# GpSimd's row sends moved between its variance sums and its root guess, in the first graph stage of a four-layer kernel

## Chip, cores and metric

One core of one Trainium2 chip runs the whole program in one launch. The metric is device time in microseconds of one execution, smaller is better.

## The reference, cut to what matters

Four layers follow each other on x of shape (32, 256, 128): a graph layer with 4 heads, a routed feed-forward layer (top 2 of 8 experts per token), a second graph layer, and a second routed layer. Each adds its output to x. The change is in the first graph layer and in the hand-over of its result to the routed layer.

```python
x = x + _L0_gnn_ref(_layernorm(x, axis=-1), adj, ...)
x = x + _L0_ffn_ref(_layernorm(x, axis=-1), L0_ffn_Wg, ...)
...
# _L0_gnn_ref
X = _heads(lrelu(node_feats @ W_lin + b_lin), B, N)
q = _heads(lrelu(node_feats @ W_q), B, N)
k = _heads(lrelu(node_feats @ W_k), B, N)
att = sigmoid(einsum('bhxd,bhyd->bhxy', q, k) * scale)
adj_h = adj_matrix[:, None] * att
deg = sum(adj_h, axis=-1)
dis = where(deg > 0, deg ** (-0.5), 0.0)
Y = einsum('bhxy,bhyd->bhxd', dis[..., :, None] * adj_h * dis[..., None, :], X)
return layernorm(Y) * ln_g + ln_b
# _L0_ffn_ref
gate_scores = x @ Wg + bg
_, idx = jax.lax.top_k(gate_scores, 2)
```

## The kernel before, in words

All engines' programs are written out by hand; semaphores alone order them. The first graph stage is a software pipeline over the 32 batches of 256 nodes (two tiles of 128 rows, TB = 2). It runs slots s = -5 to 31. In slot s, batch s gets its scores and its weighted adjacency matrix, while other batches stand at other steps: batch s-2 its output, s-4 its attention term added to x, s-6 its normalised rows, s-7 its gates.

Names that the prediction uses, by engine.

- VectorE (DVE), `gnn0_vector`. Its order in a slot is the body of the loop over s: `xd` (L937) and `xs` (L944) weigh the values; `veps` (L956) takes the degrees; `adj_h` (L908, twice) weighs the adjacency matrix; `y_sb` (L951) weighs the output; `kqT` (L919) finishes keys and queries. Between them the generator `solve_steps` is advanced by `next(steps)`. It turns variances and degrees of the slot before into reciprocal roots for all three layer norms and the degrees at once, on tiny tiles of 16 columns: `newt` (L865, L868), `near` and `far` (L871, L872, L875), `rstd` (L884), `dis` (L887), `shift` (L891). A second generator, `picks`, is advanced beside it: the choice of two experts per token and the row numbers of a group (`gmax`, `place`, `chosen`, `pair`, `emask`, `row_of`). The `bn_stats` (L897) measure mean and variance of two tiles each: of the input batch s+5, of `y_sb` of batch s-2, and of the rows of batch s-4 after the attention term was added (`AT_R`, written to `stats` from `xres`).
- GpSimd (POOL), `gnn0_gpsimd`. In each slot: `sums_of_stats` (seven ops of 8 or 16 columns: `mdiff`, `sqsum`, `mdiff`, `sqsum`, `veps`, `guess`, `msum`, L1242 to L1255) once the slot before has all its statistics; then `send` of one tile; then `add_attention` (three ops of 256 columns on `y_n` and `xres`, L1226, L1229, L1232); then `send` of another tile. DVE's `newt` L865 waits for `guess`; its `bn_stats` of the rows of batch s-4 wait for `add_attention`.
- A send (L1262) is an indirect DMA: 128 normalised rows from `rows` go to the places `row_of` in the DRAM tensor `pair_rows`. A group is four batches, so eight tiles in four parts of two. The groups 0 to 3 are sent one part per slot: tile 0 of the part behind the attention term of one slot, tile 1 ahead of the attention term of the next. Group 4 (IN_DRAIN - 1) is sent four tiles at a time at the end of slots 30 and 31. Groups 5 and up follow after the loop.
- ScalarE (ACT), `gnn0_scalar`, takes the sigmoid of the scores in two halves (`psum`, L687), normalises, and copies results out of PSUM (`yT` L693, `deg` L727 and others). TensorE (PE) does scores (L431), output (L493, L519), degrees (L542, L579) and values (L506).

The order around the change, as written:

```python
for s in range(FIRST, NB):
    if s > 0:
        sums_of_stats(s)
    for g, part in second_tiles(s):
        send(g, part, [1])
    if batch(s - 4):
        add_attention(s - 4)
    for g, part in sends(s):
        send(g, part, [0] if g < IN_DRAIN - 1 else range(TB))
```

## Time and profile before

| | us |
|---|---|
| median of 3 runs | 714.55 (712.74 to 719.56) |
| the profiled execution's own time | 719.42 |
| its span | 717.6 |
| PE busy in the span | 633.6 (88%) |
| DVE busy | 531.4 (74%) |
| ACT busy | 471.8 (66%) |
| POOL busy | 363.3 (51%) |

The busy times are of the whole span; the first graph stage takes about its first 265 us, and the shares there differ. A row of the timeline gives the start in us from the span's start, the duration in us, the engine, the line, the operation, output and inputs with their shapes, and in brackets the idle time before it with what ended it. Where several instructions of a line follow each other, one row holds them all (x2). Starts of consecutive DVE rows lie a little closer than the durations, since the end of one overlaps the start of the next.

### The profile page before, as it was taken

To read this page: it belongs to the slowest core of one execution; us is meant where nothing else is said; L and a number is where in the kernel's file an instruction comes from. 1 tells how busy PE (TensorE), PEld (TensorE's weight loads), DVE (VectorE), ACT (ScalarE), POOL (GpSimd) and SP (SyncE) were. 2 spreads that over 40 slices of the span, in tenths; PEclk is the share of its full clock that TensorE was granted. 3 is DMA by queue.
4 is the path that set the end of the run, shared out by engine and by line. 5 is a ranking of instruction groups with operands and counts; after the bars stand their busy time and mean duration, and the time that the engine had idled before them with its cause. 6 is when DMAs were issued, how large, how long until landed. Compare 5 with 4: busy or idle time off the path is not lost. (4 is left out here: it accounts for less than half of the span.)

```text
span 717.6 us, 18377 instructions
## 1 busy us (share of the span) xinstructions
PE 633.6 (88%) x5323; PEld 522.7 (73%) x5323; DVE 531.4 (74%) x2246; ACT 471.8 (66%) x1286; POOL 363.3 (51%) x603
## 2 busy tenths in 40 slices
PE   7799999999999786597999999996789889999984
PEld 5456665555565445586998999995788779999984
DVE  6899899999999887354443444443899951899998
ACT  6688999888888632454665666762257768666651
POOL 2144546777777872553544545454443105846530
PEclk9999999999999955698999999998999979999997
DMA  6357233544321114221673455324894101022011
GB/s 185 110 128 166 80 115 108 152 119 123 105 78 49 57 34 115 61 60 45 166 153 112 130 156 149 93 58 107 180 256 132 59 0 61 2 89 60 31 60 60
DMA packets 75796, 71.80 MB, mean 100 GB/s; under 512 B 7782, under 2 KB 64770, under 8 KB 74930
## 3 DMA queue, kind: packets, MB, share of 16 engines
q1 hardware_dynamic: 62194, 51.12, 25.3%
q0 software_dynamic: 11200, 13.35, 7.7%
q10 hardware_dynamic: 2304, 6.16, 3.2%
q8 instruction: 46, 0.75, 0.5%
q14 instruction: 52, 0.43, 0.2%
HBM read 44.06 MB, written 26.54 MB: 98 GB/s over the span
## 5 line engine op out<-in xcount | busy, mean ns | idle before, releaser
L1942 POOL DMA_INDIRECT expert_outputs<-y_rows,y_at x91 | 87.5, 962 | 96.1 <-DVE y_rows L1913 90.9
L1704 ACT ACTIVATE hT<-psum,b1blk 128x128 f32<-128x128 f32 x280 | 80.1, 370 | 41.6 <-issue 28.9
L1620 PE MATMUL psum<-xinT,w1blk 128*128 128x128 f32 x728 | 100.9, 284 | 5.4 <-ACT xinT L1689 5.4
L1642 PE MATMUL psum<-f_w,hT 128*128 x728 | 97.8, 279 | 0.0
L1620 PEld LDWEIGHTS psum<-xinT,w1blk 128*128 128x128 f32 x728 | 92.8, 200 | 6.4 <-ACT xinT L1689 6.3
L1642 PEld LDWEIGHTS psum<-f_w,hT 128*128 128x128 f32 x728 | 90.1, 195 | 0.0
L1894 DVE TENSOR_SCALAR w1blk<-f_w 128x256 f32 x182 | 47.0, 300 | 44.4 <-issue 41.9
L1262 POOL DMA_INDIRECT pair_rows<-rows,row_of x64 | 64.2, 1003 | 29.9 <-DVE row_of L1050 16.6
L908 DVE TENSOR_TENSOR adj_h<-psum,adjT 128x1024 f32<-128x1024 f32 x64 | 75.8, 1214 | 2.1 <-ACT psum L687 1.8
L687 ACT ACTIVATE psum<-psum 128x1024 f32<-128x1024 f32 x64 | 64.1, 1007 | 17.8 <-PE psum L431 16.6
L1913 DVE TENSOR_TENSOR y_rows<-psum,b2wide 128x128 f32<-128x128 f32 x91 | 26.5, 291 | 64.3 <-PE psum L1642 50.4
L2575 PEld LDWEIGHTS psum<-w2s,hT 128*128 128x128 f32 x512 | 62.3, 193 | 4.1 <-ACT hT L2647 2.5
L2575 PE MATMUL psum<-w2s,hT 128*128 128x128 f32 x512 | 62.7, 276 | 2.1 <-DVE xh L2742 2.1
L2555 PE MATMUL psum<-xh3T,w1s 128*128 128x256 f32 x256 | 63.1, 390 | 0.0
L2647 ACT ACTIVATE hT<-psum,b1sel 128x256 f32<-128x256 f32 x128 | 49.9, 466 | 9.8 <-PE psum L2555 9.8
L2833 POOL COPY w1s<-f_w 128x256 f32 x60 | 25.5, 436 | 53.4 <-issue 35.9
L2555 PEld LDWEIGHTS psum<-xh3T,w1s 128*128 128x128 f32 x256 | 47.8, 197 | 5.8 <-issue 0.2
L2636 ACT ACTIVATE w2s<-f_w,wtok 128x256 f32 x64 | 28.7, 500 | 31.0 <-PE psum L2575 30.9
L1242 POOL TENSOR_TENSOR mdiff<-stats 128x8 f32<-128x8 f32 x31 | 6.4, 205 | 77.3 <-DVE stats L897 45.4
L542 PE MATMUL psum<-adj_h,ones 128*32 128x256 f32 x512 | 35.9, 400 | 3.6 <-DVE adj_h L908 3.5
L493 PE MATMUL psum<-adj_h,xs 128*32 128x256 f32 x496 | 34.1, 392 | 4.0 <-DVE gate L962 3.9
L2374 POOL TENSOR_TENSOR xres<-xres,wb_row 128x1024 f32<-128x1024 f32 x8 | 18.9, 2357 | 36.9 <-DVE hf_scale L2305 36.9
(369 smaller groups left out, 1538.0 us busy)
## 6 DMA issues: line engine op xcount, KB each, us to landing
adj_in<-in_adj_dram SPq DMA_DIRECT2D x32, 256.0 KB
adjT_scratch<-adjT SPq DMA_DIRECT2D x32, 256.0 KB, 2.9
adjT<-adjT_scratch SPq DMA_DIRECT2D x6, 1024.0 KB
xin<-pair_rows SPq DMA_DIRECT2D x91, 64.5 KB
xres<-in_x_dram SPq DMA_DIRECT2D x16, 256.0 KB
b2wide<-b_of_blocks ACTq DMA_DIRECT2D x7, 512.0 KB
xres<-expert_outputs POOLq DMA_DIRECT2D x6, 512.0 KB, 9.6
out_dram<-yout SPq DMA_DIRECT2D x6, 512.0 KB, 3.3
```

What stands on the lines that cost most here:

```text
L542: ins = nc.tensor.matmul(psum[HD * h:HD * (h + 1), AT_BANK, 0:NN], ones[:, 0:HD], adj_h[:, b % 3, h, c, :], start=(c == 0), stop=(c == TB ...
L687: nc.scalar.activation(pair, pair, ACT.Sigmoid, scale=float(HD) ** -0.5).then_inc(s_att, 1)
L908: nc.vector.tensor_tensor(adj_h[:, b % 3, 2 * u:2 * u + 2, :, :].rearrange("p h c n -> p h (c n)"), psum[:, 2 * u:2 * u + 2, :], adjT[:, b ...
L1262: pool.indirect_dma_start(rows_dram[:, :], bass.IndirectOffsetOnAxis(ap=row_of[:, g % NROWS, t:t + 1], axis=0), rows[:, g % NROWS, t, :], ...
L1620: ins = nc.tensor.matmul(psum[:, HIDDEN_BANKS + n % 2, lo:lo + P], w1blk[:, u, k, c * P:(c + 1) * P], xinT[:, u, :], start=True, stop=True)
L1642: ins = nc.tensor.matmul(psum[:, OUT_BANKS + n % 2, 0:D], hT[:, u, k, c, :], flat[:, bass.ds(places[k] + (HID + c * D), D)], start=(k == 0 ...
L1704: ins = nc.scalar.activation(hT[:, u, k, c, :], psum[:, HIDDEN_BANKS + n % 2, lo:lo + P], ACT.Gelu, bias=first_bias[:, c, k, i:i + 1])
L1894: ins = nc.vector.tensor_scalar(w1blk[:, u, k, :], flat[:, bass.ds(places[k], HID)], 1.0, None, ALU.mult)
L1942: pool.indirect_dma_start(y_dram[:, :], bass.IndirectOffsetOnAxis(ap=y_at[:, u:u + 1], axis=0), y_rows[:, u, :], None).then_inc(s_y_sent[u ...
L2555: ins = nc.tensor.matmul(psum[:, 2 * (n % 2) + k, c * NN:(c + 1) * NN], w1s[:, n % SLOTS4, k, c * P:(c + 1) * P], xh3T[:, n * NN:(n + 1) * ...
L2575: ins = nc.tensor.matmul(psum[:, 4 + n % 2, r * P:(r + 1) * P], hT4[:, n % 2, k, c, r * P:(r + 1) * P], w2s[:, n % SLOTS4, k, c * D:(c + 1 ...
L2647: nc.scalar.activation(hT4[:, n % 2, k, c, :], psum[:, 2 * (n % 2) + k, c * NN:(c + 1) * NN], ACT.Gelu, bias=b1sel[:, c, k, n:n + 1]).then ...
```

## The change

On VectorE the `bn_stats` of the rows with the attention term move up: they now stand right behind those of `y_sb`, ahead of the four steps of `solve_steps` and `picks`. On GpSimd the function of the sums is cut in two. The first five ops start once the solution before the last is there (the wait on `s_norm` is two counts lower); both sends of the slot's part follow; then `guess` and `msum`, in a new function, with the waits on the degrees and on the last solution; then the attention term, with no send behind it. Each part of the groups 0 to 3 is sent one slot later than its first tile was. Group 4 is spread: part 0 behind the attention term of slot 30, part 1 inside slot 31's sums, part 2 behind slot 31's attention term, part 3 after the loop.

```diff
@@ gnn0_vector
                 elif s == FIRST + 3:
                     leaky(0)
+                if batch(s - 4):
+                    dve.wait_ge(s_x1, s - 3)
+                    for t in range(TB):
+                        add_stats1(s, AT_R + t, tile_at(s - 4, t))
                 for _ in range(4):
                     next(steps, None)
                     next(picks, None)
@@
                     next(picks)
                     next(picks)
-                if batch(s - 4):
-                    dve.wait_ge(s_x1, s - 3)
-                    for t in range(TB):
-                        add_stats1(s, AT_R + t, tile_at(s - 4, t))
                 next(steps, None)
@@ gnn0_gpsimd, sums_of_stats
-                pool.wait_ge(s_norm, 2 * solve_no(s) - 2)
+                pool.wait_ge(s_norm, 2 * solve_no(s) - (4 if s > 1 else 2))
...
                 nc.gpsimd.tensor_tensor(v[:, 0:NLN], mdiff[:, :], sqsum[:, :], ALU.add).then_inc(s_sums, 1)
-                pool.wait_ge(s_sums, done + 5)
+
+            def guess_of_roots(s):
...
+                pool.wait_ge(s_sums, SUMS * (s - 1) + 5)
                 pool.wait_ge(s_degmax, s)
+                pool.wait_ge(s_norm, 2 * solve_no(s) - 2)
                 nc.gpsimd.tensor_scalar(guess.bitcast(I32)[:, :], v.bitcast(I32), -0.5, RSQRT_MAGIC, ALU.mult, ALU.add)\
                     .then_inc(s_sums, 1)
                 nc.gpsimd.tensor_tensor(msum[:, :], mean_a, mean_b, ALU.add).then_inc(s_sums, 1)
...
-            def sends(s):
-                for r in range(s - GB, s):
+            def sends_first(s):
+                for r in range(s - GB - 1, s - 1):
                     g = ranks(r)
                     if g is not None and g < IN_DRAIN - 1:
-                        yield g, s - 1 - r
-                    elif g is not None and r > s - 3:
-                        for part in (2 * (s - 1 - r), 2 * (s - 1 - r) + 1):
-                            yield g, part
-            def second_tiles(s):
-                return [(g, part) for g, part in sends(s - 1) if g < IN_DRAIN - 1]
+                        yield g, s - 2 - r
+                    elif g is not None and r == s - 2:
+                        yield g, 1
+            def sends_last(s):
+                g = ranks(s - 1)
+                if g is not None and g == IN_DRAIN - 1:
+                    yield g, 0
+                g = ranks(s - 2)
+                if g is not None and g == IN_DRAIN - 1:
+                    yield g, 2
             for s in range(FIRST, NB):
                 if s > 0:
                     sums_of_stats(s)
-                for g, part in second_tiles(s):
-                    send(g, part, [1])
+                for g, part in sends_first(s):
+                    send(g, part)
+                if s > 0:
+                    guess_of_roots(s)
                 if batch(s - 4):
                     add_attention(s - 4)
-                for g, part in sends(s):
-                    send(g, part, [0] if g < IN_DRAIN - 1 else range(TB))
+                for g, part in sends_last(s):
+                    send(g, part)
...
+            send(IN_DRAIN - 1, 3)
             add_attention(NB - 4)
             send_group(IN_DRAIN)
```

VectorE's program in a middle slot, before (`stats<-xres` the second time is the one of the rows with the attention term):

```order
L897 BN_STATS stats<-y_sb 128x6 x2
L875 SCALAR_TENSOR_TENSOR near<-near,guess 128x16
L981 TENSOR_TENSOR place<-gate,gmax 128x64
L884 SCALAR_TENSOR_TENSOR rstd<-far,near 128x16
L985 TENSOR_TENSOR place<-place,power 128x64
L887 SCALAR_TENSOR_TENSOR dis<-veps,rstd 128x8
L891 SCALAR_TENSOR_TENSOR shift<-msum,rstd 128x8
L988 TENSOR_REDUCE chosen<-place 128x8
L1002 TENSOR_TENSOR pair<-chosen 128x8
L897 BN_STATS stats<-xres 128x6 x2
L937 TENSOR_TENSOR xd<-psum,dis 128x256
```

and the same slot of the changed kernel:

```order
L897 BN_STATS stats<-y_sb 128x6 x2
L897 BN_STATS stats<-xres 128x6 x2
L875 SCALAR_TENSOR_TENSOR near<-near,guess 128x16
L981 TENSOR_TENSOR place<-gate,gmax 128x64
L884 SCALAR_TENSOR_TENSOR rstd<-far,near 128x16
L985 TENSOR_TENSOR place<-place,power 128x64
L887 SCALAR_TENSOR_TENSOR dis<-veps,rstd 128x8
L891 SCALAR_TENSOR_TENSOR shift<-msum,rstd 128x8
L988 TENSOR_REDUCE chosen<-place 128x8
L1002 TENSOR_TENSOR pair<-chosen 128x8
L937 TENSOR_TENSOR xd<-psum,dis 128x256
```

Nothing is added or dropped: the two statistics moved past eight small ops of the solution and the picks.

GpSimd's program in a slot with sends, before (DMA is one send of one tile):

```order
L1242 TENSOR_TENSOR mdiff<-stats 128x8
L1243 TENSOR_TENSOR sqsum<-stats 128x8
L1245 TENSOR_TENSOR mdiff<-mdiff 128x8
L1247 TENSOR_SCALAR sqsum<-sqsum 128x8
L1250 TENSOR_TENSOR veps<-mdiff,sqsum 128x8
L1253 TENSOR_SCALAR guess<-veps 128x16
L1255 TENSOR_TENSOR msum<-stats 128x8
L1262 DMA pair_rows<-rows,row_of 236544x129
L1226 TENSOR_TENSOR y_n<-y_n,ln_g 128x256
L1229 TENSOR_TENSOR y_n<-y_n,ln_b 128x256
L1232 TENSOR_TENSOR xres<-y_n,xres 128x256
L1262 DMA pair_rows<-rows,row_of 236544x129
```

and in the changed kernel, where the new code shifts line numbers (L1260 is `guess`, L1262 now `msum`, L1269 a send):

```order
L1242 TENSOR_TENSOR mdiff<-stats 128x8
L1243 TENSOR_TENSOR sqsum<-stats 128x8
L1245 TENSOR_TENSOR mdiff<-mdiff 128x8
L1247 TENSOR_SCALAR sqsum<-sqsum 128x8
L1250 TENSOR_TENSOR veps<-mdiff,sqsum 128x8
L1269 DMA pair_rows<-rows,row_of 236544x129 x2
L1260 TENSOR_SCALAR guess<-veps 128x16
L1262 TENSOR_TENSOR msum<-stats 128x8
L1226 TENSOR_TENSOR y_n<-y_n,ln_g 128x256
L1229 TENSOR_TENSOR y_n<-y_n,ln_b 128x256
L1232 TENSOR_TENSOR xres<-y_n,xres 128x256
```

The send that stood behind the attention term now stands, with the other one, ahead of `guess`.

## Rows read from the trace of the kernel before

**Rows 1.** Windows: stretch, its us, busy PE, PEld, DVE, ACT, POOL, PEclk, DMA, GB/s
```profile
76.00:119.00 43.00, 41.60 (x438) 26.28 (x434) 40.60 (x155) 38.87 (x85) 22.41 (x60) 1.00 0.35 105
126.20:242.60 116.40, 107.10 (x1091) 66.55 (x1094) 112.47 (x395) 99.13 (x211) 88.83 (x181) 1.00 0.33 101
```
**Rows 2.** Timeline, DVE: `kqT` opening four slots
```profile
75.67 0.68 DVE L919 TENSOR_TENSOR kqT<-psum,raw 128x512 f32<-128x512 f32 x1
...
118.95 0.68 DVE L919 TENSOR_TENSOR kqT<-psum,raw 128x512 f32<-128x512 f32 x1
...
126.23 0.68 DVE L919 TENSOR_TENSOR kqT<-psum,raw 128x512 f32<-128x512 f32 x1
...
242.67 0.68 DVE L919 TENSOR_TENSOR kqT<-psum,raw 128x512 f32<-128x512 f32 x1
```
**Rows 3.** Groups by line, DVE, 76 to 119 us (no sends): busy, mean ns
```profile
L865 DVE SCALAR_TENSOR_TENSOR newt<-guess 128x16 f32<-128x16 f32 x6 | 1.0, 166 | 0.0
L868 DVE TENSOR_TENSOR newt<-newt,veps 128x16 f32<-128x16 f32 x6 | 0.9, 157 | 0.0
```
**Rows 4.** Groups by line, DVE, 126.2 to 242.6 us (sends)
```profile
L868 DVE TENSOR_TENSOR newt<-newt,veps 128x16 f32<-128x16 f32 x15 | 6.3, 421 | 0.1
L865 DVE SCALAR_TENSOR_TENSOR newt<-guess 128x16 f32<-128x16 f32 x15 | 6.1, 408 | 0.0
```
**Rows 5.** Timeline, DVE, one slot with sends
```profile
149.56 0.68 DVE L919 TENSOR_TENSOR kqT<-psum,raw 128x512 f32<-128x512 f32 x1
150.15 0.39 DVE L865 SCALAR_TENSOR_TENSOR newt<-guess 128x16 f32<-128x16 f32 x1
...
150.87 0.49 DVE L868 TENSOR_TENSOR newt<-newt,veps 128x16 f32<-128x16 f32 x1
...
152.00 0.15 DVE L875 SCALAR_TENSOR_TENSOR near<-near,guess 128x16 f32<-128x16 f32 x1
...
153.00 0.48 DVE L897 BATCH_NORM_STATS2 stats<-xres 128x6 f32<-128x128 f32 x2
...
153.85 0.43 DVE L944 SCALAR_TENSOR_TENSOR xs<-xd 128x256 f32<-128x256 f32 x1
...
157.06 0.43 DVE L951 TENSOR_TENSOR y_sb<-psum,dis 128x256 f32<-128x256 f32 x1 [0.34 <-PE psum L519]
```
**Rows 6.** Timeline, POOL, the same slot
```profile
150.60 0.73 POOL L1232 TENSOR_TENSOR xres<-y_n,xres 128x256 f32<-128x256 f32 x1
151.47 1.01 POOL L1262 DMA_INDIRECT pair_rows<-rows,row_of  x1
153.57 0.20 POOL L1242 TENSOR_TENSOR mdiff<-stats 128x8 f32<-128x8 f32 x1 [1.09 <-DVE stats L897]
...
153.97 0.37 POOL L1245 TENSOR_TENSOR mdiff<-mdiff 128x8 f32<-128x8 f32 x1
...
154.72 0.20 POOL L1250 TENSOR_TENSOR veps<-mdiff,sqsum 128x8 f32<-128x8 f32 x1
...
155.65 1.04 POOL L1262 DMA_INDIRECT pair_rows<-rows,row_of  x1 [0.15 <-issue]
...
158.35 0.73 POOL L1232 TENSOR_TENSOR xres<-y_n,xres 128x256 f32<-128x256 f32 x1
```
**Rows 7.** Timeline, POOL, sends in a row, then unhindered sums
```profile
244.69 1.01 POOL L1262 DMA_INDIRECT pair_rows<-rows,row_of  x1 [0.16 <-issue]
246.00 0.96 POOL L1262 DMA_INDIRECT pair_rows<-rows,row_of  x1 [0.30 <-issue]
...
249.52 0.22 POOL L1242 TENSOR_TENSOR mdiff<-stats 128x8 f32<-128x8 f32 x1
...
250.42 0.20 POOL L1250 TENSOR_TENSOR veps<-mdiff,sqsum 128x8 f32<-128x8 f32 x1
```
**Rows 8.** Timeline, DVE and POOL: attention term at its latest
```profile
235.33 0.62 DVE L865 SCALAR_TENSOR_TENSOR newt<-guess 128x16 f32<-128x16 f32 x1
...
236.19 0.59 DVE L871 SCALAR_TENSOR_TENSOR near<-newt 128x16 f32<-128x16 f32 x1
...
236.00 0.75 POOL L1232 TENSOR_TENSOR xres<-y_n,xres 128x256 f32<-128x256 f32 x1
```

**Rows 9.** Waits, 118 to 242 us: us in total, times, longest us
```profile
POOL mdiff L1242 <- DVE stats L897: 16.5, 16, 1.4
...
ACT psum L687 <- PE psum L431: 8.0, 12, 1.1
```

More of the change, by code:

```diff
@@ L1250, in sums_of_stats @@
                 nc.gpsimd.tensor_tensor(v[:, 0:NLN], mdiff[:, :], sqsum[:, :], ALU.add).then_inc(s_sums, 1)
-                pool.wait_ge(s_sums, done + 5)
+            def guess_of_roots(s):
+                was = (s - 1) % 2
+                mean_a, mean_b = (stats[:, was, :, i] for i in (1, 4))
+                v = veps[:, was, :]
+                pool.wait_ge(s_sums, SUMS * (s - 1) + 5)
                 pool.wait_ge(s_degmax, s)
+                pool.wait_ge(s_norm, 2 * solve_no(s) - 2)
                 nc.gpsimd.tensor_scalar(guess.bitcast(I32)[:, :], v.bitcast(I32), -0.5, RSQRT_MAGIC, ALU.mult, ALU.add)\
@@ L1255, in sums_of_stats, with send @@
                 nc.gpsimd.tensor_tensor(msum[:, :], mean_a, mean_b, ALU.add).then_inc(s_sums, 1)
-            def send(g, part, tiles=range(TB)):
-                if part == 0 and tiles[0] == 0:
+            def send(g, part):
+                if part == 0:
                     pool.wait_ge(s_rows, g + 1)
                     pool.wait_ge(s_tokens, g + 1)
-                for t in (part * TB + t for t in tiles):
+                for t in range(part * TB, (part + 1) * TB):
                     pool.indirect_dma_start(
```

## Prediction

> **What bounds the kernel now.** I read the windows first, for the engine that is full where the change is. In the stretch of the first graph stage without sends, DVE is busy 40.60 of 43.00 us and PE 41.60; in the one with sends, DVE is busy 112.47 of 116.40 us (97%), PE 107.10, GpSimd 88.83, at a granted clock of 1.00 in both [rows 1]. So with sends DVE sets the pace and GpSimd has about a quarter of its time to spare. The timeline of DVE then gives the slot's length, from one `kqT` to the next: six slots from 75.67 to 118.95 us make 7.21 us each, fifteen from 126.23 to 242.67 us make 7.76 [rows 2]. The 0.55 us more, in 16 slots some 8.5 us, are what the sends cost today. Nothing of it is a wait on a send.
>
> The groups by line say where it sits. `newt` L865 takes 166 ns without sends and 408 with; `newt` L868 takes 157 and 421 [rows 3, 4]. That is 0.24 + 0.26 = 0.51 us per slot, nearly the whole difference. The timelines of the two engines side by side show why. `kqT` starts at 149.56. `newt` L868 starts at 150.87 and ends at 151.36; GpSimd's last attention op runs from 150.60 to 151.33 [rows 5, 6]. DVE's tiny op ends 0.03 us after GpSimd's big one: it was held by it. The send behind the attention term, from 151.47, holds nothing: DVE's `near` at 152.00 takes its usual 0.15. So the quantity that matters is how late after `kqT` the attention term ends; call it A. Here A = 151.33 - 149.56 = 1.77 us, and 0.39 + 0.49 - 0.17 - 0.16 = 0.55 us are lost. At the latest one in the loop (`kqT` at 234.73, reckoned as 0.60 before its `newt`) A = 236.75 - 234.73 = 2.02, and 0.62 + 0.59 - 0.34 = 0.87 are lost [rows 8]. Between the two, 0.25 us of A cost 0.32 us of DVE. For no loss A would have to be under about 0.7 us, where `newt` starts 0.60 us into the slot [rows 5].
>
> **The change part by part.** What it changes is A. I work it out for the slot of rows 5 and 6.
>
> The statistics move up past eight small ops: from 153.00 to 152.00 in this slot, so GpSimd may start its sums 1.00 us earlier [rows 5]; it now waits 1.09 us for them, so it will [rows 6]. In the other kinds of slot fewer or other picks stand there; I take 0.95. The statistics themselves are no longer or shorter.
>
> From the first sum to the attention's end takes GpSimd 159.08 - 153.57 = 5.51 us now, with one send in it [rows 6]. Both sends will be in it. A second send right behind a first starts 246.00 - 244.69 = 1.31 us later [rows 7], so the chain becomes 5.51 + 1.31 = 6.82 us. Against that, today's sums are themselves stretched by DVE: `veps` starts 1.15 us after the first sum here, 0.90 where DVE stood idle [rows 6, 7]. If the stretch goes, the chain is 6.57.
>
> A changes by -0.95 + 1.31 = +0.36 us, or by +0.11 without the stretch. A slot that gets longer delays sums and next `kqT` alike, so this is no runaway. Removing the send behind the attention term gives nothing: GpSimd then only waits longer for the statistics, as it does already (16 waits before `mdiff`, 16.5 us together [rows 9]). I take +0.13, near the unstretched end, because the sums now lie beside ops of some 0.16 us instead of beside `xs` with 0.43 [rows 5]; both ends stay for the range. At 0.32 / 0.25 that is 0.17 us of DVE in a slot. In the slot of rows 5 DVE waited 0.34 us for PE before `y_sb`, so some of it is hidden there; ScalarE waits for the scores 12 times, up to 1.1 us [rows 9], and I put some five or six of the 16 slots down to that chain. For about 10 slots: **+1.7 us**. The ends are 10 x 0.14 = +1.4 and 16 x 0.46 = +7.4; below, if GpSimd starts and ends so that a `newt` slips in ahead, -0.1 in a slot, -1.6.
>
> Sums beside the solution. The five small GpSimd ops now run while DVE does `near`, `rstd`, `dis`, `shift` and the picks, ops of the kind that was held. No row shows a small GpSimd op holding a small DVE op. From below: a held op ended 0.03 us behind the holder, and its own 0.16 overlap it, so a 0.20 us op can delay another by 0.20 + 0.03 - 0.16 = 0.07, five of them by 0.35 us in a slot. From above nothing speaks for a gain: the ops beside the sums today, `xs` with 0.43 us, are not held. I take zero, near what `xs` shows; 21 slots on the path would cost up to +7.4.
>
> The Trainium skill, page "SBUF — State Buffer", section "Who interferes with whom", puts the rule more harshly: a DVE instruction with two SBUF inputs and a GpSimd one that reads SBUF take a shared pair of ports in order of issue, and the first holds it for the whole instruction. The traces agree on the attention ops (held until 0.03 us after). By that rule each small sum of 0.20 us could cost its full length, and the sum would come out on the slower side; that is a rival below. The rule also says that statistics, with one SBUF input, are never held, so moving them would change nothing by itself; the rows agree.
>
> The `guess` comes later. It would end about 0.90 + 0.36 + 1.31 + 0.99 + 0.20 = 3.8 us after the first sum, which starts 0.57 us behind the start of the statistics [rows 5 to 7]: 152.00 + 0.57 + 3.8 = 156.4, and `newt` needs it at 158.0 (`y_sb` at 157.06, 0.34 to `kqT`, 0.60 more). The cover is 1.6 us; costed at nothing, and if GpSimd ran over, a slot would grow by the overrun. The waits that `guess` gets (degrees, last solution) are over by then: `veps` of the degrees is written right after `xs`, at 154.3. Behind `guess` are queued `msum` and the attention ops only.
>
> The wait of DVE's statistics on the attention term is reached 1.00 us earlier, 152.00 instead of 153.00, and the term ends at 151.33, later 151.46: 0.5 us of cover. Behind that wait would stand the whole solution.
>
> The end of the loop: the sums of slot 31 no longer stand behind four sends (rows 7 show the first two), but DVE's `newt` there was not late for `guess`. The last attention term stands behind as many sends as before. Nothing. Slots 1 to 14 have no sends, their attention term ends before `newt` already (166 ns, rows 3), and ends 0.9 us sooner to no use.
>
> The sum: 0 + 1.7 + 0 = +1.7 us. I shade it by 0.5, since the attention term may slip past one `newt`: **+1.2 us**. Against the profiled execution, 719.42 + 1.2 = 720.6. The median of the runs shown is 4.87 lower, and a difference of this kind carries over: 714.55 + 1.2 = **715.7 us**. About 1%, 7 us, is what a measurement of this kernel can tell from no change.
>
> **The rivals.**
>
> Relief. The aim may be met: the attention term leaves `newt` alone and slots with sends go to 7.21 us. 16 x 0.55 = -8.8, **705.7 us**. For it: the sums start 1 us sooner. Against it: 1.31 us come in ahead of the attention term for the 1 us won. A must fall by 1.07 us, and 1.31 of added chain excludes that unless both sends together take about 1.2 us instead of 2.3.
>
> A small relief. If two sends behind the sums cost GpSimd less than 1.31 us, or some attention ops wait for DVE instead of the other way, A falls by 0.1 to 0.2: 16 x 0.17 = -2.7, **711.8 us**.
>
> Slower, held by the sums. Each small sum holds the ports for its whole 0.20 us, and DVE's solution loses half of five such ops, 0.5 us a slot, in the 21 slots from the first picks on: +10.5 us, **725.1 us**. It decides from 0.34 us a slot on. For it: attention ops hold DVE to their very end. Against it: `xs` is not lengthened beside `mdiff` L1245; it is GpSimd's op that takes 0.37 [rows 5, 6]. DVE had started first there, though.
>
> Slower by the full shift. A rises by 0.36, and DVE loses 0.46 us in ten to sixteen slots: about +6, **720.6 us**, still within 1%.
>
> No effect: the change only moves spare time of GpSimd and DVE loses 0.55 as before, **714.6 us**.
>
> **How the numbers follow.** Chances: the forecast with no effect beside it (-1.5 to +4 us) 0.66; small relief 0.12; relief 0.05; full shift 0.10; held by the sums 0.07. The full shift has a fifth of its chance beyond 7 us, the others none across their bound: faster by over 1% 0.05, slower by over 1% 0.07 + 0.02 = 0.09, within 1% 0.86. The range must hold 0.8: from the small relief, less 1.8 for the spread of medians of a few runs (the three shown differ by 6.8), to the full shift plus 1: 710 to 721.6 us.
>
> **What would show it.** Right: in the changed profile `mdiff` L1242 starts 0.57 us behind the start of the moved statistics, A stands at 1.8 to 2.0 us in slots with sends, the two `newt` still take about 0.4 us each, and slots with sends last 7.7 to 8.0 us. Slots without sends stay at 7.2. The step on A is wrong if the two `newt` fall to 0.17; the step on the sums is wrong if `near`, `rstd`, `dis` and `shift` take visibly more than 0.16 or slots without sends grow. An idle time of DVE before `newt` or before the moved statistics would show that the cover of 1.6 or 0.5 us was not there. The forecast as a whole is wrong beyond 7 us either way.

## The result, and the profile after

The changed kernel takes 721.35 us, median of 22 runs (718.36 to 728.16); the kernel before, run beside it 22 times, 717.04 us (712.74 to 721.38). The ratio is 1.0057, with a 95% interval of 1.0037 to 1.0078: the change costs 4.1 us (2.7 to 5.6). That is within 1%, on the slower side, and some 3 us more than forecast. The profiled execution took 722.68 us, its span 721.0, against 719.42 and 717.6 of before.

The windows of the two stretches, after (columns as in [rows 1]):

```profile
76.00:119.00 43.00, 41.84 (x432) 26.02 (x430) 40.60 (x154) 39.31 (x84) 20.54 (x60) 1.00 0.35 106
126.20:242.60 116.40, 102.25 (x1042) 63.82 (x1042) 104.99 (x376) 95.27 (x204) 82.87 (x174) 1.00 0.33 100
```

The reader is to see that DVE no longer fills the stretch with sends: 104.99 of 116.40 us (90%), where it had 112.47 (97%) in [rows 1]. The granted clock is 1.00 as before. The slots, from `kqT` to `kqT`, are these (timeline of DVE, after):

```profile
127.47 0.68 DVE L919 TENSOR_TENSOR kqT<-psum,raw 128x512 f32<-128x512 f32 x1
...
160.67 0.68 DVE L919 TENSOR_TENSOR kqT<-psum,raw 128x512 f32<-128x512 f32 x1
...
169.12 0.68 DVE L919 TENSOR_TENSOR kqT<-psum,raw 128x512 f32<-128x512 f32 x1
...
249.38 0.68 DVE L919 TENSOR_TENSOR kqT<-psum,raw 128x512 f32<-128x512 f32 x1
```

Fifteen slots take 249.38 - 127.47 = 121.91 us, 8.13 each; they were 7.76 [rows 2]. The first of them starts 1.24 us later than before (127.47 against 126.23), and the slot behind the last of them 6.71 later (249.38 against 242.67). The hand-over to the routed layer takes some of it back: its first row load starts 5.0 us later, and the span ends 3.4 us later.

Now what DVE does with its time. Groups by line of the stretch with sends, after:

```profile
L951 DVE TENSOR_TENSOR y_sb<-psum,dis 128x256 f32<-128x256 f32 x15 | 6.4, 425 | 9.7 <-PE psum L519 9.4 <-issue 0.3
L937 DVE TENSOR_TENSOR xd<-psum,dis 128x256 f32<-128x256 f32 x14 | 5.9, 425 | 0.8 <-DVE shift L891 0.8
L868 DVE TENSOR_TENSOR newt<-newt,veps 128x16 f32<-128x16 f32 x15 | 4.4, 291 | 0.1
L865 DVE SCALAR_TENSOR_TENSOR newt<-guess 128x16 f32<-128x16 f32 x15 | 4.3, 287 | 0.0
L884 DVE SCALAR_TENSOR_TENSOR rstd<-far,near 128x16 f32<-128x16 f32 x14 | 2.8, 197 | 0.1
```

The two `newt` take 287 and 291 ns; they took 408 and 421 [rows 4]. So DVE got 0.25 us of each slot back (both `newt` together take 0.58 us, where they took 0.83), the relief that I had given a small chance. But in front of `y_sb` it now stands idle for 9.7 us, waiting for TensorE's L519. The waits of 118 to 242 us, after, say what lies behind that:

```profile
POOL mdiff L1242 <- DVE stats L897: 21.5, 15, 2.3
ACT yT L693 <- PE psum L493: 10.5, 14, 1.3
DVE y_sb L951 <- PE psum L519: 9.4, 14, 1.0
```

ScalarE's `yT` waits 10.5 us for TensorE's L493 (3.7 before), and L519, which multiplies `yT`, comes late for DVE (9.4; 3.1 before). The timeline of one slot, after, shows it:

```profile
163.43 0.21 POOL L1242 TENSOR_TENSOR mdiff<-stats 128x8 f32<-128x8 f32 x1 [1.19 <-DVE stats L897]
164.77 1.16 POOL L1269 DMA_INDIRECT pair_rows<-rows,row_of  x1 [0.15 <-issue]
165.68 1.07 PE L493 MATMUL psum<-adj_h,xs 128*32 128x256 f32 x16 [0.16 <-DVE gate L962]
166.24 0.98 POOL L1269 DMA_INDIRECT pair_rows<-rows,row_of  x1 [0.31 <-issue]
166.68 0.70 PE L509 MATMUL psum<-xhT,w_c 128*128 128x256 f32 x2
167.29 0.20 POOL L1260 TENSOR_SCALAR guess<-veps 128x16 int32<-128x16 int32 x1
167.59 0.38 ACT L693 ACTIVATE yT<-psum 128x256 f32<-128x256 f32 x1 [1.15 <-PE psum L493]
168.78 0.42 DVE L951 TENSOR_TENSOR y_sb<-psum,dis 128x256 f32<-128x256 f32 x1 [0.98 <-PE psum L519]
169.35 0.74 POOL L1232 TENSOR_TENSOR xres<-y_n,xres 128x256 f32<-128x256 f32 x1
```

L493's sixteen products start at 165.68 and end at 166.75 by the records, and the next matmul, L509, starts on time. Yet `yT` starts at 167.59, 1.91 us behind L493's start. In slots without sends it is 1.13 us wherever nothing else holds `yT`. I call L493's start + 1.13 the time at which `yT` is due; here it is 0.78 late. Over the fifteen slots the distance is 1.65 us in the mean, 1.21 to 1.91; it was 1.18 before. One slot nearly escaped (0.08 late), with the same sends at the same distance; timeline, after:

```profile
229.69 1.16 POOL L1269 DMA_INDIRECT pair_rows<-rows,row_of  x1 [0.15 <-issue]
230.59 1.07 PE L493 MATMUL psum<-adj_h,xs 128*32 128x256 f32 x16 [0.16 <-DVE gate L962]
231.15 0.98 POOL L1269 DMA_INDIRECT pair_rows<-rows,row_of  x1 [0.31 <-issue]
231.80 0.38 ACT L693 ACTIVATE yT<-psum 128x256 f32<-128x256 f32 x1 [0.29 <-PE psum L493]
```

That slot lasts 7.60 us. The two slots that come nearest to it in build, with `yT` 0.78 and 0.77 late, last 8.45 and 8.47, but they also hold one pair of `bn_stats` more, and L493 starts 0.16 to 0.18 us later in them. So some 0.7 of the 0.86 us go with the late `yT`. Two theories went to the chip. **Held result:** a send of GpSimd beside TensorE's work delays the moment from which others see that work as done; this ate the relief. **Bubble:** the loss is on DVE itself, because the statistics no longer lie between `shift` and `xd`, and the sums now lie beside the solution.

### The profile page after: what moved, and what is told of

Read it like the earlier page. It is cut to its first block and busy times, and to the rows that moved or that the text cites. A ratio compares the mean times of both kernels' runs of the same rounds, so it can differ in the third digit from the quotient of the medians.

```text
span 721.0 us, 18377 instructions
## 1 busy us (share of the span) xinstructions
PE 632.3 (88%) x5323; PEld 520.1 (72%) x5323; DVE 521.8 (72%) x2246; ACT 473.0 (66%) x1286; POOL 355.7 (49%) x603
## 5 line engine op out<-in xcount | busy, mean ns | idle before, releaser
L1269 POOL DMA_INDIRECT pair_rows<-rows,row_of x64 | 64.5, 1008 | 32.1 <-issue 16.1
L687 ACT ACTIVATE psum<-psum 128x1024 f32<-128x1024 f32 x64 | 64.1, 1007 | 16.5 <-PE psum L431 14.6
L1718 ACT ACTIVATE hT<-psum,early_b 128x128 f32<-128x128 f32 x84 | 24.0, 371 | 21.6 <-PE psum L1634 12.0
L431 PE MATMUL psum<-kqT 32*128 32x256 f32 x512 | 37.6, 408 | 0.3 <-DVE kqT L919 0.3
```

The lines of the kernel that those rows point to most:

```text
L431: ins = nc.tensor.matmul(psum[:, h, c * NN:(c + 1) * NN], kqT[rows_h, b % 2, 0, c * P:(c + 1) * P], kqT[rows_h, b % 2, 1, :], start=True, ...
L687: nc.scalar.activation(pair, pair, ACT.Sigmoid, scale=float(HD) ** -0.5).then_inc(s_att, 1)
L1269: pool.indirect_dma_start(rows_dram[:, :], bass.IndirectOffsetOnAxis(ap=row_of[:, g % NROWS, t:t + 1], axis=0), rows[:, g % NROWS, t, :], ...
L1718: ins = nc.scalar.activation(hT[:, u, k, c, :], psum[:, HIDDEN_BANKS + n % 2, lo:lo + P], ACT.Gelu, bias=first_bias[:, c, k, i:i + 1])
```

## The experiments

All ratios are against runs of the kernel before on the same chip, with the 95% interval. Where "one execution" is written, the kernel does extra work in a few slots and ran once; only these slots are read, and its time is not compared. "Slot" is the mean from `kqT` to `kqT` over the fifteen slots with sends, A the end of the attention term behind `kqT`, "newt" both ops together; before has 7.76, 1.78 and 0.83 us.

**One half at a time: statistics alone.**

```diff
@@ gnn0_vector of the kernel before
+                if batch(s - 4):
+                    ... the statistics of AT_R, moved up from behind the picks
                 for _ in range(4):
                     next(steps, None)
```

> The kernel before with one edit: DVE's statistics of the added rows stand ahead of the four solution steps; GpSimd is as before. Theory 'late completion' (the changed kernel loses because its sends run beside TensorE's output products L493 and ScalarE's yT then starts 0.4 to 0.7 us late): here the sends stay at the two sides of the attention term, at about +0.3 to +2 and +5 us after kqT, partly ahead of and partly behind L493, so yT should follow the first L493 by 1.2 us in most slots; GpSimd's sums start some 0.5 to 0.9 us earlier (2.9 to 3.4 after kqT instead of 3.9), A falls to 0.8 to 1.4, and slots with sends fall below 7.76 us: 3 to 6 us faster than before. Theory 'bubble' (the loss comes from DVE, since statistics no longer lie between shift and xd, and xd waits 0.6 to 0.8 us for shift): that wait is fully here, in about 26 slots, so this kernel is as slow as the changed one or slower, +4 us against before.

Measured: 717.91 against 717.47 us, ratio 0.9989 (0.9957 to 1.0021). Slot 7.69, A 1.36, newt 0.64. The bubble is fully there (`xd` waits 0.8 us in all for `shift` in 118 to 242 us, just as after), and the kernel is not slower: that theory carries little. But the 3 to 6 us of gain did not come either. A fell by 0.42 only, so the two `newt` kept most of their stretch (0.64 of 0.83 us), and of the 0.19 us that they gave back the slots show 0.07. A part of the rest is likely lost at the first sigmoid, as the timeline of a slot shows; how much, no run separates:

```profile
135.07 1.15 PE L431 MATMUL psum<-kqT 32*128 32x256 f32 x16
135.27 1.01 POOL L1262 DMA_INDIRECT pair_rows<-rows,row_of  x1 [0.16 <-issue]
136.61 1.01 ACT L687 ACTIVATE psum<-psum 128x1024 f32<-128x1024 f32 x1 [0.77 <-PE psum L431]
```

The attention term ends earlier, so the send behind it starts earlier and now lies over the scores L431. The first sigmoid, otherwise 1.18 us behind L431's start, comes at 1.54, which is 1.34 us behind the send's start. It is 0.13 to 0.38 late in all fourteen slots with a send 0.98 to 1.26 us ahead of its due time. The same hold in another place.

In the same run it does not reach every reader. `raw` (L699) is ScalarE's copy of what L509 makes:

```profile
131.68 1.04 POOL L1262 DMA_INDIRECT pair_rows<-rows,row_of  x1 [0.21 <-issue]
132.04 0.70 PE L509 MATMUL psum<-xhT,w_c 128*128 128x256 f32 x2
132.78 0.60 ACT L699 ACTIVATE raw<-psum 128x512 f32<-128x512 f32 x1 [0.22 <-PE psum L509]
```

It waits for TensorE, the send starts 1.10 us ahead of it, and it is on time, 0.74 us behind L509 as in the slots without sends.

**The other half: GpSimd's part alone.**

```diff
@@ gnn0_vector of the changed kernel
-                if batch(s - 4):
-                    ... the statistics of AT_R
                 for _ in range(4):
...
+                if batch(s - 4):
+                    ... the statistics of AT_R
                 next(steps, None)
```

> The changed kernel with DVE's statistics back at their old place, behind the four solution steps; GpSimd's part as changed (both sends between the sums and the guess). By either theory worse than the changed kernel: the sums cannot start before about 3.9 after kqT, the attention term ends 1.0 to 1.3 us later than in the changed kernel (A about 2.2 to 3), both newt stay stretched to 0.4 us or more, and the statistics at +3.3 begin to wait for the attention term. Slots with sends 8.3 to 9 us, 8 to 18 us slower than before. 'Late completion' expects yT still late where a send lies beside L493 (sends at about 5 to 6.5, L493 at 5.0): 1.5 to 1.9 us behind the first L493. 'Bubble' expects the wait of xd for shift to be gone and yT not to matter, hence at most +4.

Measured: 729.53, ratio 1.0163 (1.0109 to 1.0217). Slot 8.64, A 2.74, newt 0.89. As expected; the cost here is the attention term, up to 3.7 us into the slot. `yT` is held in three slots of fourteen only; most first sends start just 0.65 us ahead of its due time. The bubble's forecast (at most 4 us slower) missed.

**Early sums, sends where they were.**

```diff
@@ gnn0_gpsimd of the kernel before, with the statistics moved up as above
-                pool.wait_ge(s_norm, 2 * solve_no(s) - 2)
+                pool.wait_ge(s_norm, 2 * solve_no(s) - (4 if s > 1 else 2))
...
                 pool.wait_ge(s_degmax, s)
+                pool.wait_ge(s_norm, 2 * solve_no(s) - 2)
```

> Both parts of the change that bring GpSimd's sums forward (statistics moved up, the first five sums started on the solution before the last), but the sends where they were before: one tile behind guess and msum, one behind the attention term. 'Late completion': sums at 2.4 after kqT, attention term over at about 0.2 to 0.6 without the second send in the chain, newt at 0.17 to 0.2 us; the one send in the chain starts at about 4.8 after kqT and lies beside L493, so yT may still be 0.3 us late in some slots, but DVE has slack for that; slots with sends 7.3 to 7.5 us, 4 to 7 us faster than before, and 8 to 11 faster than the changed kernel. 'Bubble': xd waits for shift as in the changed kernel, so no better than the changed kernel less its attention overlap: within 2 us of before.

Measured: 718.21, ratio 1.0018 (0.9987 to 1.0049). Slot 7.78, A 1.35, newt 0.76. A miss for "held result" as I had put it. Two reasons in the trace: the first sigmoid is 0.07 to 0.37 late again in all fourteen slots with a send 0.97 to 1.28 us ahead of its due time, and the chain did not get shorter. `guess` waits for the degrees that DVE writes behind `xs`: in the slot that starts at 149.88 it starts 4.98 us behind `kqT`, though the last sum ended at 4.16. 0.8 us of GpSimd lie idle there, and the send behind it is paid in full.

**Both sends behind the guess.**

```diff
@@ gnn0_gpsimd of the changed kernel
-                for g, part in sends_first(s):
-                    send(g, part)
                 if s > 0:
                     guess_of_roots(s)
+                for g, part in sends_first(s):
+                    send(g, part)
```

> The changed kernel with both sends behind guess and msum instead of between the sums and guess; everything else as changed. 'Late completion': the sends move from +4.1 and +5.5 to about +5.1 and +6.4 after kqT, where L493 (records end at about +5.9) is under the first send and the sums of the degrees and the next scores L431 (+1.4) are beside its tail; yT still late where the first send starts before L493 ends, about half the slots, and scores late in others; A unchanged at 0.9 to 1.7. So 0 to 2 us faster than the changed kernel. A rival 'late guess' (the guess behind both sends holds newt): guess now ends 2 us earlier, and the gain is only as large as the wait of newt for guess was, which is zero in the trace: the same time as the changed kernel within 1 us.

Measured: 728.88, ratio 1.0162 (1.0115 to 1.0209). Slot 8.46, A 2.60, `yT` at 1.13 to 1.23 behind L493 in every slot. Both expectations missed: the hold was gone and it was still slower. GpSimd's timeline of this kernel says why:

```profile
165.23 0.20 POOL L1250 TENSOR_TENSOR veps<-mdiff,sqsum 128x8 f32<-128x8 f32 x1
166.58 0.20 POOL L1260 TENSOR_SCALAR guess<-veps 128x16 int32<-128x16 int32 x1 [1.15 <-issue]
167.29 1.02 POOL L1269 DMA_INDIRECT pair_rows<-rows,row_of  x1 [0.21 <-issue]
168.61 0.97 POOL L1269 DMA_INDIRECT pair_rows<-rows,row_of  x1 [0.30 <-issue]
```

From the last sum to `guess` 1.15 us are idle, for the degrees, and the chain from the first sum to the attention term's end takes 7.64 us in this slot, against 6.66 in the changed kernel's. A send ahead of the guess would fit into that hole, so the change's idea may have worth, for one send of the two.

**Sends and fills where there are none.**

```diff
@@ gnn0_gpsimd of the changed kernel, between sums and guess
+                if 4 <= s < 8:
+                    try_send()
+                    try_send()
+                elif 8 <= s < 12:
+                    try_set()
+                    try_set()
```

> The changed kernel with extra GpSimd work between its sums and its guess in slots where it sends nothing: slots 4 to 7 two extra indirect sends of 128 zero rows to a scratch tensor that nothing reads, slots 8 to 11 two fills of 128 x 1024 values (no DMA), slots 12 and 13 nothing. Its output is the same; it does extra work. 'Late completion by the send': in slots 4 to 7 yT starts 1.5 to 1.9 us behind the first record of L493 instead of 1.13 to 1.3, in slots 8 to 11 it keeps 1.13 to 1.3. 'GpSimd busy time' (any long GpSimd work there delays the chain through the guess or the attention term): both kinds show the same delay. 'Order of work on TensorE' (yT is late because y_sb of the slot and degrees stand in another order): neither shows it.

Measured, one execution: of the four slots with two extra sends, two can show nothing, since ScalarE is busy until `yT` starts; in one `yT` is 1.04 late (2.17 behind L493), in the other on time. In the four slots with two fills it follows L493 by 1.12 or 1.13 us each time. In all eight the attention term came later, A 0.8 to 2.4. So a fill costs time but held nothing; a send can.

One send, plain DMAs, or two sends behind the attention term, in the same manner:

> The changed kernel with extra GpSimd work in slots where it sends nothing: slots 4 to 6 one extra indirect send between sums and guess, slots 7 to 9 two plain (not indirect) DMAs issued from GpSimd there, slots 10 to 13 two extra indirect sends behind the attention term (so at about +0.2 to +2.5 of the next slot, beside the scores L431). All go to a scratch tensor that nothing reads. 'Late completion by the send': one send delays yT only if it lies over L493 (start at +4.0, records of L493 from +4.3: 0.3 to 0.6 us late); the plain DMAs delay nothing if it is the making of descriptors by GpSimd, and the same if it is the data moved; sends behind the attention term delay the first sigmoid from 1.18 us behind L431's first record to 1.8 us. If instead it is the place behind the sums alone, slots 10 to 13 show no delay at the sigmoid.

Measured, one execution: two slots with one send whose start lies 1.8 us ahead of `yT`'s due time: on time. The plain DMAs showed nothing, but they lay 1.4 us or more ahead, and `yT` had 0.19 us of cover, so this says little. Two sends behind the attention term: the first sigmoid 0.77, 0.73, 0.56 and 0.40 late, the slots 7.98, 7.94, 7.82 and 7.76 us long. The hold goes with the send to another consumer, as expected.

**Fills for sends, in four slots.** Otherwise the changed kernel.

```diff
-                    send(g, part)
+                    if g == 1:
+                        fill(g)
+                    else:
+                        send(g, part)
```

> The changed kernel, but in the four slots of group 1 (the fourth to seventh full slot with sends, 153 to 185 us in the changed kernel) GpSimd fills a tile of 128 x 1340 values twice where it sent twice, about the same 1.3 us each and no DMA; the eight sends of group 1 stand together behind the attention term of the last of these slots, whose successor is long for that reason. 'TensorE held by the send': in the four slots yT follows the first L493 by 1.13 to 1.2 us (1.5 to 1.9 with sends), and they last 7.5 to 7.7 us instead of 7.71, 8.45, 7.76 and 8.58. 'GpSimd's time' (what costs is that the chain is long, whatever fills it): the slots keep their length of 7.7 and 8.5 us.

Measured, one execution: 7.17, 7.77, 7.38 and 8.07 us for the four slots, where the changed kernel has 7.71, 8.45, 7.76 and 8.58: 0.53 us less in the mean. The second of them in the timeline (its lines stand two further down than the changed kernel's: L495 is L493, L695 is L693):

```profile
163.17 2.37 POOL L1299 MEMSET try_fill<- 128x1340 f32 x2
164.30 1.07 PE L495 MATMUL psum<-adj_h,xs 128*32 128x256 f32 x16 [0.16 <-DVE gate L964]
165.43 0.38 ACT L695 ACTIVATE yT<-psum 128x256 f32<-128x256 f32 x1 [0.42 <-PE psum L495]
165.63 0.20 POOL L1262 TENSOR_SCALAR guess<-veps 128x16 int32<-128x16 int32 x1
```

GpSimd is as busy as with two sends (2.37 us against 2.45), A behind the four slots is 1.2 to 1.8 (0.8 to 1.7 with sends), and `yT` comes 1.13 us behind L493. The slots of the same execution that still send behave as in the changed kernel (7.79 and 8.62 us ahead of the four, `yT` 0.37 and 0.56 late). "Held result" stands, with its size in these four slots: 0.53 us a slot.

**A scan of the distance.**

```diff
@@ gnn0_gpsimd of the changed kernel, behind the attention term
+                if 4 <= s < 14:
+                    columns, count = SCAN[s - 4]
...
+                    nc.gpsimd.memset(try_fill[:, 0:columns], 0.0).then_inc(s_tryc, 1)
...
+                    for _ in range(count):
+                        try_send()
```

> The changed kernel with extra work in slots 4 to 13, where it sends nothing: behind the attention term a fill of 64 to 2150 columns and then one extra send (slots 4 to 8) or two (slots 9 to 13) to a scratch tensor that nothing reads. The fill shifts the send against the scores L431. 'TensorE held': with one send, the first sigmoid is late where it would have started 0.9 to 1.35 us behind the send's start, and then starts at the send's start + 1.36; it is on time (1.18 us behind the first L431) where it would start at over 1.4 us. With two sends it starts at about +2.1 or +2.8 of the first one where it would have fallen shortly before. 'Descriptor queue' (the send delays by a fixed amount whenever it lies within 2 us): the same delay at every distance.

Measured, one execution. With one send the first sigmoid was due 1.65, 1.22, 1.15, 1.14 and 0.93 us behind the send's start, and came 0, 0.13, 0.24, 0.23 and 0.44 late, that is at 1.35 to 1.39 behind the send's start whenever it was due sooner. With two sends, due 2.74, 2.50, 2.22, 1.93 and 1.89 behind the first one, it came 0.66, 0.87, 0.71, 1.02 and 1.05 late: at 2.93 to 3.40. The last row of the one-send part in the timeline (lines four further down: L435 is L431, L691 is L687):

```profile
76.06 1.15 PE L435 MATMUL psum<-kqT 32*128 32x256 f32 x16
76.31 1.03 POOL L1301 DMA_INDIRECT try_rows<-pad_rows,try_row  x1 [0.15 <-issue]
77.68 1.01 ACT L691 ACTIVATE psum<-psum 128x1024 f32<-128x1024 f32 x1 [0.85 <-PE psum L435]
```

For one send the forecast of the theory holds to 0.03 us. For two, the releases at 2.1 and 2.8 that I had read off the changed kernel do not carry over; a fixed delay at every distance is excluded too.

**What in the send does it.** The same place, with `try_plain()`, nothing, or a send of 32 or 128 rows behind the fill.

> The changed kernel with extra work in slots 4 to 13, where it sends nothing, behind the attention term: a fill of 860 to 2150 columns, then in slots 4 to 8 one plain DMA of 128 rows issued by GpSimd, in slot 9 nothing, in slots 10 to 12 an indirect send of 32 rows, in slot 13 one of 128 rows. All go to a scratch tensor that nothing reads. By the scan before, an indirect send of 128 rows that starts 0.9 to 1.3 us ahead of the time at which the first sigmoid is due delays it until 1.36 us behind the send's start. If it is GpSimd's making of scattered descriptors, plain DMAs at the same distance delay nothing, and 32 rows delay less than 128 (release under 1.36 us). If it is the issue of any GpSimd DMA, all three kinds delay alike. Slot 9, with the fill alone, shows the first sigmoid on time, 1.18 us behind the first L431.

Measured, one execution, lines four further down. Plain DMAs 1.02, 1.03, 0.88 and 0.89 us ahead of the due time: none late (a fifth, 1.50 ahead, neither). The fill alone: on time. 32 rows, 1.45, 0.89 and 0.76 ahead: 0, 0.40 and 0.55 late. 128 rows, 1.14 ahead: 0.17 late. One of each kind:

```profile
71.15 1.15 PE L435 MATMUL psum<-kqT 32*128 32x256 f32 x16
71.45 0.59 POOL L1308 DMA_DIRECT2D try_rows<-pad_rows  x1
72.33 1.01 ACT L691 ACTIVATE psum<-psum 128x1024 f32<-128x1024 f32 x1 [0.41 <-PE psum L435]
...
107.50 1.15 PE L435 MATMUL psum<-kqT 32*128 32x256 f32 x16
107.92 0.90 POOL L1302 DMA_INDIRECT try_rows<-pad_rows,try_row  x1 [0.16 <-issue]
109.23 1.01 ACT L691 ACTIVATE psum<-psum 128x1024 f32<-128x1024 f32 x1 [0.96 <-PE psum L435]
```

The number of rows hardly matters: with 32 rows the release lies 1.29 and 1.31 us behind the start. That it takes the indirect kind is likely, but not quite shown. The record of a plain DMA is 0.59 us long, that of a send 1.01, and sends release 0.3 to 0.4 us behind the end of their record. If a plain DMA did the same, it would release at 0.9 to 1.0, and only the two at 0.88 and 0.89 could show it, by 0.1 us at most. None was late, but no plain DMA was tried closer.

**The version that follows.** One send in the hole ahead of the guess, the other behind the attention term, the statistics and the wait as changed.

```diff
@@ gnn0_gpsimd of the changed kernel
                 for g, part in sends_first(s):
-                    send(g, part)
+                    send(g, part, [0] if g < IN_DRAIN - 1 else range(TB))
                 if s > 0:
                     guess_of_roots(s)
                 if batch(s - 4):
                     add_attention(s - 4)
+                for g, part in sends_first(s):
+                    if g < IN_DRAIN - 1:
+                        send(g, part, [1])
```

> The changed kernel with one of the two sends of a part kept between the sums and the guess, and the other back behind the attention term. The guess waits for the degrees, at about 4.9 after kqT, in any case, so the first send (4.0 to 5.3) costs the chain almost nothing. Theory 'TensorE held': TensorE's finished work is seen late when it ends up to about 1.3 us behind the start of a GpSimd send. Here L493 would be finished 1.3 to 1.8 us behind the first send and the scores 1.5 us behind the second (from about +1.0), so yT follows L493 by 1.13 to 1.2 us and the first sigmoid L431 by 1.18 us; A falls to 0.7 to 1.1, the two newt to 0.17 to 0.3 us; slots with sends 7.3 to 7.5 us, 4 to 7 us faster than the kernel before. Rival 'attention term': only A counts; then the same slots, since A is low, but yT may be late without harm. Rival 'bubble' (xd waits for shift because the statistics stand ahead): slots keep 7.6 to 7.8 us and the time is that of the kernel before.

Measured: 711.57 against 716.46 us, ratio 0.9919 (0.9892 to 0.9947): 5.8 us faster than before (3.8 to 7.7). Slot 7.34, A 0.57, newt 0.39, `yT` 1.16 behind L493 in the mean. Groups by line, and the timeline of one slot from `kqT` at 156.51:

```profile
L865 DVE SCALAR_TENSOR_TENSOR newt<-guess 128x16 f32<-128x16 f32 x16 | 3.7, 233 | 0.0
L868 DVE TENSOR_TENSOR newt<-newt,veps 128x16 f32<-128x16 f32 x16 | 2.5, 159 | 0.1
```

```profile
156.58 0.75 POOL L1232 TENSOR_TENSOR xres<-y_n,xres 128x256 f32<-128x256 f32 x1
157.47 1.01 POOL L1269 DMA_INDIRECT pair_rows<-rows,row_of  x1
160.34 1.16 POOL L1269 DMA_INDIRECT pair_rows<-rows,row_of  x1 [0.15 <-issue]
161.25 1.07 PE L493 MATMUL psum<-adj_h,xs 128*32 128x256 f32 x16 [0.16 <-DVE gate L962]
161.57 0.20 POOL L1260 TENSOR_SCALAR guess<-veps 128x16 int32<-128x16 int32 x1
162.37 0.38 ACT L693 ACTIVATE yT<-psum 128x256 f32<-128x256 f32 x1
```

In this slot both sends start over 1.36 us ahead of the two readers that were held so far: 2.04 before `yT`'s due time, 1.59 before the first sigmoid's. Of the fifteen slots only the first has its sigmoid late, by 0.20. The hold is not gone, though: in five slots ScalarE's `xh1T` (L721), a copy of what L554 makes, starts 0.43 to 0.50 us late, 1.34 to 1.43 behind a send. Those slots last 7.18 to 7.23 us, so it costs nothing there. `newt` L868 is back at 159 ns, the 157 of slots without sends [rows 3].

**What of it is needed.** The version above, once with the statistics back at the old place, once with the old wait:

```diff
@@ gnn0_gpsimd, sums_of_stats, the second of the two
-                pool.wait_ge(s_norm, 2 * solve_no(s) - (4 if s > 1 else 2))
+                pool.wait_ge(s_norm, 2 * solve_no(s) - 2)
```

> The kernel with one send between the sums and the guess and one behind the attention term, but with DVE's statistics of the added rows back behind the four solution steps. If the earlier statistics are what lets the attention term end in time, the sums start at about 3.3 to 3.9 after kqT again, the chain from the sums to the attention term's end stays at 5.5 to 5.8 us, A is 1.2 to 1.8 and both newt stay stretched to 0.3 or 0.4 us: slots with sends 7.5 to 7.8 us, within 3 us of the kernel before, that is 3 to 6 us slower than with the statistics moved. If the place of the send ahead of the guess alone were what counts, it would be as fast as that kernel.

> The kernel with one send between the sums and the guess and one behind the attention term and the statistics moved up, but the sums wait for the last solution again instead of the one before the last. They then start about 0.1 us behind the end of shift, at 3.0 to 3.3 after kqT instead of 2.4 to 2.6; the first send starts at 4.7 and lies closer to L493, whose finish is 0.9 to 1.2 us behind it, so yT is 0.2 to 0.4 us late in some slots; the guess starts at about 6.0 and A is 1.2 to 1.5. Slots with sends 7.5 to 7.7 us: 2 to 5 us slower than with the relaxed wait, 0 to 4 us faster than the kernel before. If the relaxed wait is to no use, both are equal within 1 us.

Measured: 719.02, ratio 1.0011 (0.9987 to 1.0034), slot 7.74, A 1.75; and 717.75, ratio 0.9989 (0.9964 to 1.0013), slot 7.70, A 1.05, with `yT` 1.47 to 1.52 behind L493 in every second slot. Each part left out takes nearly the whole gain away, the second one partly through the hold.

## Why the prediction was right or wrong

The side and the bound were right: slower, within 1%. The way there was wrong, and 4.1 us is 3 times the 1.2 forecast. That the side came out right was luck: the two largest effects, sends that hold TensorE's results (an estimated +8 us) and the relief of `newt` (-3.8), stood in no term of the sum, and they offset each other. The time itself, 721.35, lies 5.7 us above the forecast 715.7 and just inside the range that ended at 721.6; 2.5 of the 5.7 come from the base, 717.04 in 22 runs where three had given 714.55. Of the signs named, the sums did follow the moved statistics by 0.55 us (162.88 to 163.43), but A was 1.40 and not 1.8 to 2.0, the two `newt` took 0.29 us and not about 0.4, and the slots 8.13 and not 7.7 to 8.0.

- **What bounds the kernel**: right. DVE's stretched `newt` cost what [rows 3, 4] said: where they shrank (one send first, by 0.44 us) the slots shrank with them, by 0.42, from 7.76 to 7.34. (0.55 us in 16 slots are 8.8 us, not 8.5.)
- **The shift of A, +0.13**: wrong in sign; A fell by 0.38, from 1.78 to 1.40. A is where the sums start, plus the chain from there to the attention term's end, less the slot's length. By the means of the fifteen slots whose sums lead to these ends, the chain grew by 1.15 us, inside the 1.06 to 1.31 forecast. The sums start 2.72 us behind `kqT` where they started at 3.90, that is 1.19 earlier, not 0.95; a less stretched `newt` pulls the statistics forward as well. And "a slot that gets longer delays sums and next `kqT` alike" is false: the slots grew by 0.35, behind the sums, at `yT`, and that comes off A (-1.19 + 1.15 - 0.35 = -0.39, which is the 0.38 but for rounding). A would have fallen without the hold too: with fills for its sends, the slot that starts at 160.67 in the changed kernel leaves A at 1.42, where before had 1.75.
- **The place of the sends beside TensorE**: the step that was missing. I checked what the sends do to GpSimd's queue and to DVE, and never what TensorE does at +4.1 to +6.5 us. With fills in four slots it measured 0.53 us a slot; for all fifteen, as an estimate, 15 x 0.53 = 8 us. With the relief of `newt` (15 x 0.25 = 3.8 less) and 0.09 a slot left over, 7.76 - 0.25 + 0.09 + 0.53 = 8.13. The trace of before had the clue: I saw ScalarE's waits for the scores [rows 9] and put five or six slots down to "that chain". Five of them are slots in which the first sigmoid is late beside a send, by 0.26 to 0.74 us.
- **Sums beside the solution, zero**: nearly right. `rstd` went from 165 to 197 ns, `dis` from 161 to 168, `shift` from 159 to 164: 0.04 us a slot, inside the bounds, far from the 0.5 of "held by the sums". By the Trainium skill, page "SBUF — State Buffer", section "Who interferes with whom", a DVE op with two SBUF inputs and a GpSimd op that reads SBUF contend for shared ports, and whichever came first holds them for its whole length. The attention ops do so here (0.73 us long); the short sums (0.20) lengthened `rstd` by 0.03 us in the mean, and nothing by more. That the statistics are not held, as the prediction has it from that section, its rows did not show, but the trace of before does: `bn_stats` beside an attention op take 276 ns in the mean (24 of them), the others 280. The same section says that TensorE and ScalarE never wait on anyone. ScalarE does wait here for TensorE's results, 0.4 to 1.0 us too long beside an indirect send; the section is on SBUF's ports, and no run here tells whether a port is what holds.
- **Statistics "no longer or shorter", and slots without sends "stay at 7.2"**: nearly. They had hidden the latency from `shift` to `xd`. Eleven slots before the sends grew by 0.73 us together, which I had costed at nothing.
- **The covers**: the 1.6 us of `guess` held (`newt` L865 never waited). The 0.5 of the statistics' wait held but for slot 16, where the attention term ended 2.5 us into the slot and the slot took 9.10.
- **The sends behind the attention term "give nothing"**: right for the queue, but the second send's cost is decided by where it lands.

Of the rivals, "relief" had the right mechanism for DVE. Its exclusion ("1.31 of added chain") overlooked that sums started early leave GpSimd idle until the degrees are there, so that one send ahead of `guess` is nearly free. None of the rivals had the hold.

## What to carry to other kernels

When a transfer is moved on one engine, list what every other engine finishes in the 1.4 us behind its new start (up to 3.4 us behind the first of two sends in a row), not only what its own queue and its port neighbour do, and read in the trace which of it comes late, since here some readers were held and others not. Look for idle time ahead of a waiting instruction (here the guess, waiting for the degrees) and put just as much there as fits: one send gained 5.8 us with its two helpers, two lost 4.1. And test halves: each half of this change alone was worth nothing or less, and the version that won loses nearly all its gain when either of its two helpers is taken out.

## What the hardware showed that I had not expected

- An indirect DMA issued by GpSimd can delay when ScalarE sees TensorE's result. Over all traces of this case, the first sigmoid (behind L431) and `yT` (behind L493), both due when sixteen matmuls are done, were late in all 47 waits in which a single send had started 0.88 to 1.28 us ahead of their due time; they came 1.27 to 1.39 us behind the send's start, with 32 rows as with 128. With 1.45 us or more, none of 38 was late. Fills of about the same length (eight slots) did nothing, nor did four plain DMAs of GpSimd 0.88 to 1.03 us ahead. TensorE's own records are not longer, and its next matmul starts on time.
- Closer than 0.88 us the hold is not certain. At 0.76 to 0.86 us one of five was held; at 0.53 to 0.73, four of fourteen first sigmoids in the kernel before, and five of eight with one send first and the old statistics. Of the fifteen pairs of the changed kernel one held next to nothing (0.08), and the same pairs, at the same distances, held nothing in twelve slots of the three kernels that tried extra work with one or two sends and with 32 rows. With pairs the release lay 2.1 to 3.4 us behind the first.
- Not every reader is held. `raw` (L699, behind the two products of L509) was on time in 26 of 28 waits with a single send 0.88 to 1.28 us ahead, and 0.10 late at most in the others; DVE's `y_sb` (behind L519) in all seven such waits of the kernel before. `xh1T` (L721, behind the two products of L554) was held five times in the version with one send first. Beside pairs, `y_sb` came 0.20 to 0.30 us late in eight slots of the kernel with GpSimd's part alone.
- What decides it stays open, and so does what is late: the matmuls, the signal of their end, or the reader. The ends of matmuls are modelled in these records.
